# Filler products on TensorE in an expert search and ahead of a spread

## What is computed

```python
def _L0_ffn_ref(x, Wg, W1, W2, W3):          # 8 experts, capacity 512 of 4096 tokens
    scores = (x_flat @ Wg.T).T
    top_vals, token_idx = jax.lax.top_k(scores, capacity)
    token_w = jax.nn.softmax(top_vals, axis=-1)
    xg = x_flat[token_idx]
    h = silu(einsum('eic,ehc->eih', xg, W1)) * einsum('eic,ehc->eih', xg, W3)
    y = einsum('eih,ech->eic', h, W2) * token_w[..., None]
    ...
def _L1_ffn_ref(x, w_gate, w_up, w_down):    # act_qdq: 16-bit steps of the tensor's largest value
    x = act_qdq(x)
    up = act_qdq(x @ lpbq_dequant(w_up).T)
    gate = act_qdq(x @ lpbq_dequant(w_gate).T)
    sig = fixed_qdq_u16(sigmoid(gate))
    gate = act_qdq(gate * sig)
    o = act_qdq(gate * up)
    return o @ lpbq_dequant(w_down).T
x = x + _L0_xattn_ref(_layernorm(x), ctx_1024, W, b)
x = x + _L0_ffn_ref(_layernorm(x), Wg, W1, W2, W3)
x = x + _L1_xattn_ref(_layernorm(x), ctx_1024, ctx_1024, mask, W_out)
x = x + _L1_ffn_ref(_layernorm(x), w_gate, w_up, w_down)
```

## Time and profile before

| | |
|---|---|
| median of 3 runs | 755.82 us (755.79 to 755.91) |
| the profiled execution | 754.42 us |
| its span, first to last instruction | 752.6 us |
| busy TensorE / VectorE / ScalarE / POOL | 641.6 / 621.7 / 529.7 / 305.9 us |
| mean granted clock of TensorE | 0.938 of 2.4 GHz |

### The profile page before, as it was taken

One profiled execution on the slowest core, in us unless ns is written; L12 is line 12 of the kernel. 1 busy time (PEld: TensorE's weight loads), 2 busy tenths in 40 slices (PEclk: granted clock), 3 DMA queues, 4 the chain that ended last, 5 costly groups with the idle time before them and its releaser, 6 DMA issues.

```text
span 752.6 us, 12183 instructions
## 1 busy us (share of the span) xinstructions
PE 641.6 (85%) x4268; PEld 386.0 (51%) x4268; DVE 621.7 (83%) x1304; ACT 529.7 (70%) x713; POOL 305.9 (41%) x249
## 2 busy tenths in 40 slices
PE   6883049999999789999999999989999995029998
PEld 5762025666666544456455645644444443006887
DVE  5898897989898699886888877988997998995433
ACT  2134664776774649898998986666657996996873
POOL 5345616577774436451343110015412443892000
PEclk9997559999999999999999999999999998559999
DMA  9946665567753580000040001021103412101443
GB/s 311 331 135 208 212 168 161 123 159 187 188 110 38 100 268 1 2 22 1 1 155 30 2 29 45 13 84 57 57 0 119 162 70 98 56 0 57 153 129 112
DMA packets 59542, 78.17 MB, mean 104 GB/s; under 512 B 7904, under 2 KB 48224, under 8 KB 59488
## 3 DMA queue, kind: packets, MB, share of 16 engines
q1 hardware_dynamic: 49936, 60.58, 24.3%
q0 software_dynamic: 7872, 14.82, 9.0%
q10 hardware_dynamic: 1680, 2.08, 0.8%
HBM read 50.07 MB, written 27.39 MB: 103 GB/s over the span
## 4 chain that ended last, share of the span: by engine, by line
PE 58%; DVE 17%; ACT 10%; POOL 2%; issue 2%; DMA 1%; DVEq 0%; POOLq 0%; ACTq 0%
PE bank L2586 11%; PE bank L2319 8%; PE bank L2260 8%; PE bank L2618 5%; PE bank L1597 4%; PE bank L1654 4%; PE bank L1639 3%; PE bank L1707 3%; DVE above L852 2%; PE bank L1669 2%; DVE qx L1320 2%; PE bank L1612 2%; PE bank L1678 2%; PE bank L1634 2%; ACT wgateT L2209 1%
## 5 line engine op out<-in xcount | busy, mean ns | idle before, releaser
L1320 DVE TENSOR_REDUCE qx<-bank 128x4 f16<-128x616 f32 x128 | 98.0, 801 | 21.7 <-PE bank L1597 20.2
L1453 ACT ACTIVATE x<-bank,bic 128x512 f32<-128x512 f32 x160 | 104.6, 690 | 15.9 <-PE bank L1639 12.1
L2260 PE MATMUL bank<-ux,uwh 128*128 128x512 f16 x384 | 91.2, 380 | 0.4 <-ACT ux L2154 0.3
L2260 PEld LDWEIGHTS bank<-ux,uwh 128*128 128x128 f16 x384 | 37.4, 98 | 45.9 <-issue 0.8
L1597 PE MATMUL bank<-Kb,qTb 128*128 128x308 bf16 x256 | 52.6, 297 | 2.0 <-DVE qx L1320 1.1
L2260 PE MATMUL bank<-ux,uwl 128*128 128x512 f16 x192 | 49.3, 379 | 0.0
L1245 POOL CAST qx<-q 128x1024 f16<-128x1024 f32 x8 | 8.5, 1066 | 98.0 <-PE bank L1612 87.3
L1639 PE MATMUL bank<-qT,K 128*128 128x512 f16 x128 | 44.4, 380 | 0.3
L2319 PE MATMUL bank<-uwh,oh 128*128 128x256 f16 x192 | 43.4, 273 | 0.3 <-ACT oh L2232 0.2
L2267 PE MATMUL bank<-uwh 128*128 128x512 f16 x46 | 12.5, 424 | 36.4 <-DVE peak L1990 36.4
L2539 ACT ACTIVATE wgateT<-bank,qs 128x512 f32<-128x512 f32 x32 | 21.9, 686 | 30.5 <-PE bank L2586 30.3
(11 more groups left out here) (464 smaller groups left out, 1887.1 us busy)
## 6 DMA issues: line engine op xcount, KB each, us to landing
x_dram<-x SPq DMA_DIRECT2D x4, 1024.0 KB, 5.3
xr<-in_w1T SPq DMA_DIRECT2D x8, 512.0 KB, 4.0
xr<-in_w3T SPq DMA_DIRECT2D x8, 512.0 KB, 4.9
xr<-in_w2T SPq DMA_DIRECT2D x8, 512.0 KB, 6.7
row_dram<-xn SPq DMA_DIRECT2D x8, 512.0 KB, 3.2
x_dram<-xr SPq DMA_DIRECT2D x8, 512.0 KB, 2.9
x<-x_dram SPq DMA_DIRECT2D x8, 512.0 KB, 4.6
xT<-in_xT SPq DMA_DIRECT2D x7, 512.0 KB, 6.6
```

The source lines that it names most:

```text
L1320: dve.tensor_reduce(qx[:, k, g * GH:(g + 1) * GH, MROW].rearrange("p (u h) -> p u h", u=2), pair[i][:].rearrange("p (u x) -> p u x", u=2)[ ...
L1453: act.activation(dst, S_[u % 2], ACT.Exp, bias=bic[:, s // 2, int(tail):int(tail) + 1], scale=1.0 / 16).then_inc(p_done, 1)
L2260: mm = pe.matmul(bank[j][:, m * TB:(m + 1) * TB], w[:, c * HI + cols:c * HI + cols + P], x[:, part, c * TB:(c + 1) * TB], start=(w is uwh ...
```

## The change

It adds `filled(n, at)` to `search_tensor`: n products of the 128 x 128 identity by itself, in fp32, into an unused piece of PSUM. Nobody reads them. Five stand ahead of the first product, three, two and one in each of the ten rounds, the latter two behind a wait for the round's first and second count. More stand between the following products up to `listed(1)`. In `ffn_tensor` the 16 fillers ahead of `spread(2, 2)` become 8, 6 and 5, behind waits for the 21st, 22nd and 23rd of the gate's 24 pieces.

```diff
+                def filled(n, at):
+                    for _ in range(n):
+                        pe.matmul(at, ident, ident, start=True, stop=True)
+
+                searching, listing = bank[3][:, 512:512 + P], bank[1][:, 0:P]
+                filled(5, searching)
                 pe.wait_ge(d_cnt, 1)
                 pe.matmul(bank[1][:, 0:1], blk16[:], cnt0[:], start=True, stop=True).then_inc(d_pe, 1)
                 for n in range(DIGITS + 1):
                     levels = LEVELS if n < DIGITS else 1
+                    if n < DIGITS:
+                        filled(3, searching)
+                        pe.wait_ge(d_cnt, LEVELS * n + 2)
+                        filled(2, searching)
+                        pe.wait_ge(d_cnt, LEVELS * n + 3)
+                        filled(1, searching)
                     pe.wait_ge(d_cnt, LEVELS * n + levels + 1)
...
                 pe.wait_ge(d_act, 1)
                 halves(bank[2], ex)
+                filled(5, searching)
                 pe.wait_ge(d_mid, 4)
                 pe.matmul(bank[3][:, 0:2], tri16[:], sums[:], start=True, stop=True)
                 pe.matmul(bank[3][:, 2:4], blk16[:], sums[:], start=True, stop=True).then_inc(d_sum, 1)
+                filled(2, searching)
                 pe.wait_ge(d_place, 1)
                 pe.wait_ge(e_wh, 1)
                 pe.matmul(squares, ones16[:], sums16[:, 0:2], start=True, stop=True).then_inc(e_sum, 1)
+                filled(6, listing)
                 pe.wait_ge(d_mid, 5)
                 halves(bank[0], slot)
+                filled(4, listing)
+                pe.wait_ge(d_hot, 1)
+                filled(4, listing)
+                pe.wait_ge(d_hot, 2)
+                filled(1, listing)
...
                 listed(0)
+                filled(3, listing)
+                pe.wait_ge(d_hot, 5)
+                filled(1, listing)
                 listed(1).then_inc(d_sum, 1)
...
                         spread(1, 2)
-                for _ in range(16):
-                    pe.matmul(bank[3][:, 0:P], ident, ident, start=True, stop=True)
+                for left, n in ((3, 8), (2, 6), (1, 5)):
+                    pe.wait_ge(k_p, FT - left)
+                    for _ in range(n):
+                        pe.matmul(bank[3][:, 0:P], ident, ident, start=True, stop=True)
                 spread(2, 2)
```

## The result

The changed kernel took 758.0 us (median of 10 runs, 755.99 to 759.48), the kernel before 756.01 us on the same chip (10 runs, 755.4 to 756.82). The ratio is 1.0022 with a 95% interval of 1.0014 to 1.003: slower by 0.2%, +2.0 us between the medians and +1.7 by the ratio. The forecast was 756.3, +0.5. The profiled execution of the changed kernel took 756.64 us against 754.42 before (+2.2).

A forecast was written before the change was run, and what follows sets the result against it. VectorE carries the search's chain, with TensorE's clock mattering little, so the gain is small. Terms +1.6 - 0.3 - 0.33 - 0.4 = +0.5 us on the median 755.82 gave 756.3 us; range 754.4 to 757.9.

The forecast's parts named there:

- The case that I gave 0.72: Whole kernel: the changed time is the same within about 0.2%, 1.5 us; chance 0.72.
- The five fillers, +1.6: Start of the search: five fillers at 1.2 GHz delay the first product by 1.61 us, counted in full; bounds +0.53 and +1.61.
- size of a filler: All filler places: one filler takes 0.217 us at 2.4 GHz and 0.43 us at 1.2 GHz.
- rival 1: Start of the search: the first fillers run at 2.4 GHz and cost +0.53; total -0.5, 755.3 us; chance 0.20.
- The clock back from 69 us and then kept: Search and lists: the clock returns to 2.4 GHz from about 69 us and stays, with 1.30 us of fillers per 2.56 us round.
- Rounds, -0.03 each: Search: a round's two products gain 0.03 us at the higher clock, 0.3 us over 11; ends 0 and 2.2.
- rival 2: Search rounds: short products gain much more, towards 0.20 us a pair; total -1.4, 754.4 us; chance 0.10.
- Rival 3: Search: the clock falls back between rounds and fillers outlast rounds by 0.2 to 0.3 us; +2.1, 757.9 us; chance 0.15.
- Lists, -0.33: Lists: second list product gains 0.15, spread 0.05, last list product no longer held by kept_warm(4) 0.13; ends 0.2 and 0.5.
- so it is passed on: Behind the lists: TensorE works back to back to the first expert at an unchanged clock, passing on the lists' 0.33 us.
- `spread(2, 2)`, -0.4: Ahead of and in spread(2, 2): if the clock is kept, transposes and product take 0.38 instead of 0.58 us each; gain 0.40.
- The signs I had named: Profile: forecast wrong if first product by 67.0, PEclk 0.50 between 70 and 110 us, or a round changes over 0.1 us.

The follow-up runs named there:

- five_alone: The kernel before with only the five fillers added ahead of the first product of the search; 757.89 us, ratio 1.0029, +2.25 us.
- tail_unfilled: The changed kernel without the 14 warm products between the last spread and the first expert; 759.94 us, ratio 1.0005 to the kernel before.
- no_five: The changed kernel without the five fillers ahead of the first product of the search; 755.87 us, ratio 1.0007 to the kernel before.
- changed_again: The changed kernel itself, unaltered, run again in the third group; 760.25 us, ratio 1.0023 to the kernel before.
- handover_filled: The changed kernel with two more warm products ahead of the last list product and two ahead of the last spread; 757.59 us, ratio 1.0034 to the kernel before.
- denser: The changed kernel without the five, round fillers only from the fifth round, denser fillers in lists and ahead of the gate's spread; 757.68 us, ratio 0.9986 to before.
- denser_again: The kernel of denser, unaltered, run again in the third group; 757.48 us, ratio 0.9997 to the kernel before.
- dense_lists_gate: The kernel of denser without any fillers in the rounds of the search; 760.63 us, ratio 1.0027 to the kernel before.
- the two gate kernels: The kernel before with its 16 gate fillers paced as 8, 6 and 5 (755.64 us, ratio 1.0002) or 8, 10 and 10 (758.52 us, ratio 0.9995).
- ten_alone: The kernel before with only ten fillers added ahead of the first product of the search; 762.9 us, ratio 1.0055.
- lists_alone: The changed kernel without the five fillers and those of the ten rounds, keeping list and gate fillers; 758.06 us, ratio 0.9994 to the kernel before.

## Why the prediction was right and wrong

The sign, and the piece that causes it, were right: fillers ahead of work that is ready. The size was not: +2.0 us came where I had +0.5. How the five fillers' part adds up stays open: the runs put all of it, about 2 us, on them, while both profiles of the changed kernel have the first product only 0.67 us late. On the median that the forecast started from, 755.82, the ratio gives 757.5, near the upper end of the range. The case that I gave 0.72, within 0.2%, has the result just beyond its edge; slower by more had 0.20. That it lies in the range is partly luck: in the first profile the fillers cost 0.67 us where I had 1.6, the gain at `spread(2, 2)` was missing, and 1.68 us that no term of mine held came behind the lists. The terms also add up to 0.57, which I wrote as 0.5.

**The five fillers, +1.6.** The right step. Shown by three runs: alone +2.25 us, taken out of the change +0.2, doubled +3.9. The term of the sum was low by about 0.4 us in the low-clock case, 1.74 us and 0.3 at VectorE's next steps, where I had counted 1.6 and TensorE's wait alone. My size of a filler was right: 0.217 us at 2.4 GHz gives 1.09 us for five, and the product came 0.67 us late instead of 0.53; at 1.2 GHz I had 1.61 and `five_alone` has 1.74. What was wrong is the certainty. I took the clock row of one execution of the kernel before as the clock of the changed kernel, and in that one's two profiles the fillers ran at 2.4 GHz, rival 1's mechanism at 0.20. (In `tail_unfilled`, with the same list there, they ran at 1.2.) Rival 1's time, a gain of 0.5 us, did not come even so: of the 1.03 us that it took off, search and lists gave 0.52, `spread(2, 2)` nothing, and 1.68 us came on top behind the lists.

**The clock back from 69 us and then kept.** In the changed kernel's two profiles it hadn't fallen at the start at all. Where it had, in `tail_unfilled`, it was back at 69.9 us, as forecast; in `no_five` at 72.7. It was then kept through the ten rounds in all of them but `changed_again`, which lost it at 94.9 us, behind the tenth round's product, where the last round has no fillers; `no_five` lost it at 96.6. The page's had shown that a thin stretch *can* keep it, not that it does.

**Rounds, -0.03 each.** Smaller still: 0.01 each between these two profiles, 25.18 against 25.27 us over ten. A round's first product took 0.18 us against 0.19. That was the right end of the bounds, and rival 2 (0.20 us a pair) falls. The Trainium skill ("TensorE: Matmul & The Clock Gate", Single matmul latency), by which a pair would have gained 0.02 to 0.04 us, is of the right order here; nearly all of such a product is latency that the clock doesn't shorten. Single rounds vary by up to 0.6 us from one profile to another (the tenth interval took 2.84 to 3.43 us), and the ten took 25.27, 25.86 and 26.18 us in three profiles with the list of the kernel before, which buries this.

**Rival 3, rounds held up.** It happened, but at the start alone and only where nothing had raised the clock before: 3.53 and 2.83 us in `no_five`. It isn't what slowed the change, whose first rounds kept their 2.55 us.

**Lists, -0.33.** The size was right, in part by luck. From the last round's product to the first spread it was 13.04 us for 13.41: 0.37 gained, where I had 0.15 for the list product. From the first spread to the last it was 5.83 us in both, where I had the rest: the spread on the chain took 0.71 us in both, and the wait behind `kept_warm(4)` was never on the chain. VectorE's `wl` stands there. In the kernel before it ends at 114.08 us, and the last list product ended at 113.94 (113.07 + 0.87). The chain before:

```profile
112.89 1.19 DVE wl L832
114.08 0.15 DVE ids L937
```

An earlier list product gains nothing beside it; with the change it is `wl` again, until 114.3. I had read a wait in TensorE's timeline without asking what else `ids` stood behind.

**The step that failed: behind the lists "TensorE works back to back to the first expert at the same clock as before, so it is passed on".** It didn't. The kernel before had the clock rise at 113.6 in the middle of solid work, and kept it. The changed kernel came there with a quick TensorE, which stood idle for parts of 110 to 111 and 112 to 113, and its clock fell at 115.2: +1.68 us, more than all gains together. In the profile of the changed kernel this is the larger part of the loss. The chain's rows show that the products were twice as long. That the idle gaps caused the fall is what the windows suggest, and it wasn't tested by itself. In all six profiles with the change's fillers in the lists the clock fell between 110.2 and 117.7 us; `handover_filled`, which filled the later gap, had it fall at 111.6, before its added products ran, and only `denser`, `denser_again` and `dense_lists_gate`, which filled the gap at 110 as well, kept it. That the fall makes the kernel slower in the median isn't shown: from the first spread to the first expert it was 12.4 to 13.2 us in the six, 13.3 in both profiles of `denser` with the clock kept, and 11.5 to 12.4 in the kernel before and the two gate kernels. I had worked out what each filler covers in the lists, but not what TensorE does with the time that a doubled speed sets free there.

**Passing on.** Even with the clock kept, `denser` gained nothing to be measured; in its profile the rows' transfer ended last (1.06 us of waiting). So in these profiles the stretch has two limits less than 2 us apart, and a gain of TensorE's is passed on only as far as the rows allow.

**`spread(2, 2)`, -0.4.** It failed in the changed kernel's first profile (0.59 and 0.58 us) and held in its second (0.38 and 0.38). Of seven profiles with 8, 6 and 5 fillers four kept the clock over the transposes; with 8, 10 and 10 four of four; with the 16 unpaced ones none of three. The last fillers end 1.3 us ahead of the transposes in the first form and 0.21 in the second. The condition was written down ("if the clock is kept"), but not as a chance. The Trainium skill ("TensorE: Matmul & The Clock Gate", Part 4: PE-mode transpose) says that the full clock doesn't engage for transposes; the trace disagrees again, with 0.38 us at 1.00 and 0.59 at the low clock for the same two transposes. Whether transposes by themselves would raise the clock no run shows.

**The signs I had named.** "The forecast is wrong if the first product comes at 67.0 or before": it came at 67.20, neither there nor at 68.1. "If PEclk has 0.50 between 70 and 110 us": not in the first profile, but in the second. I had named no sign for 115 us, where the loss was.

## What to carry to other kernels

Put filler products only where TensorE would wait anyway; ahead of ready work that a chain hangs on they cost their length, less what that work waits anyway, and here five of them cost more than the higher clock gave back in 50 us of search and lists. Before raising the clock, add up how much of the chain is TensorE's own long work: here 10 rounds of tiny products gained 0.1 us. Before counting an engine's wait as a gain, look at what else the next step stands behind: here it was VectorE's `wl`. And don't take the clock of one execution of the kernel before for that of the changed kernel; look also at where the quicker engine will stand idle, since the clock may go again there.

## What the hardware showed that was not expected

- The place at which the clock falls is not fixed. Ahead of the first filler, where the kernels' lists are the same, it was at 65.8 us in the kernel before, at 65.9 in `five_alone` (mean 0.93 in 65 to 66), between 62 and 63 in both profiles of `denser`, and it did not fall there at all in four: both profiles of the changed kernel, `handover_filled` and `ten_alone`. It goes with something that differed earlier. These four have TensorE wait 0.90 or 0.91 us ahead of L703, the last product of the first block; in `five_alone` and `tail_unfilled`, whose fillers ran at 1.2 GHz, it was 1.70 and 1.72, as in the kernel before. Both kernels that were profiled twice repeated their wait. It isn't the wait alone, though: `lists_alone` and `dense_lists_gate`, without these fillers, also had 0.90 us, and their clock fell at 64.4 and 67.3. So the clock that the fillers got may belong to the kernel and not to the execution; the runs don't tell these apart. Timeline of TensorE before, and in the changed kernel:

```profile
64.46 0.41 PE L703 MATMUL bank<-cst,rx 128*128 128x128 f32 x2 [1.70 <-DVE rx L599]
64.52 0.41 PE L703 MATMUL bank<-cst,rx 128*128 128x128 f32 x2 [0.90 <-DVE rx L599]
```

- A higher mean clock doesn't go with a shorter time: the changed kernel's mean granted clock was 0.967 against 0.938, and its span 2.3 us longer; in `no_five` it was 0.958 to 0.966, and the time can't be told from that before.
- The length of VectorE's small steps beside POOL's `xn` depends on how they fall: with the product 1.7 us later a cast took 0.45 us for 0.17, another step 0.28 for 0.54, and the row of them 0.28 us more. The first round interval was 3.56 to 3.61 us in all three profiles with the product that late (`five_alone`, `ten_alone`, `tail_unfilled`), for 3.29.
- In `dense_lists_gate` ScalarE started a cast 3.3 us behind its data, with no releaser on the core. In `ten_alone` and `changed_again` the same cast came 1.4 and 0.8 us later than in the kernel before. It is not explained.
